# One kernel, one change: where a batch's rows are scattered to the experts' regions

## The reference, cut to what matters

```python
x = L0_attn_x                                              # (8, 1024, 256)
x = x + _layernorm(_L0_attn_ref(_layernorm(x), ...))       # linear attention per token, 16 heads of 16
x = x + _layernorm(_L0_ffn_ref(_layernorm(x), ...))        # causal attention, then a mixture of experts

# first attention, per token: q, k = elu of the projections, v
kv1 = jnp.einsum('bshe,bshd->bsed', K1, V) * SCALE         # sum over the 16 heads
w1  = jnp.einsum('bshe,bsed->bshd', Q1, kv1)               # the same for the second halves

# second part
scores = q @ k / sqrt(HD), causal mask; ctx = softmax(scores) @ v        # 16 heads, 4 key heads
h = clip(residual + ctx @ Wo); flat = rmsnorm(h)
probs = softmax(flat @ Wr); topv, topi = top_k(probs, 2)   # 2 of 8 experts for each token
moe_out = sum over the two of topv * (silu(flat @ Wg[e]) * (flat @ Wu[e])) @ Wd[e]
out = clip(h + moe_out)
```

## Time and profile before

| | us |
|---|---|
| median of 3 runs | 4165.04 (4164.26 to 4166.23) |
| the profiled execution | 4157.04 |
| its span | 4155.2 |
| PE busy | 3078.5 (74%) |
| DVE busy | 2298.0 (55%) |
| ACT busy | 1675.9 (40%) |
| POOL busy | 1106.6 (27%) |
| POOL issuing the 128 scatters of the loop | 123.7 |
| one turn of the loop (25.99 to 429.81, 429.81 to 828.58) | 403.8, 398.8 |

### The profile page before, as it was taken

How to read it: one execution, slowest core, us unless ns; L and a number is a source line. 1 busy time by engine, 2 the same in 40 slices (tenths; PEclk the granted TensorE clock), 3 DMA queues, 4 the chain that set the end, 5 groups by cost and what they waited for, 6 DMA issues and landing times. The chain is left out here.

```text
span 4155.2 us, 54042 instructions
## 1 busy us (share of the span) xinstructions
PE 3078.5 (74%) x17636; PEld 1799.8 (43%) x17637; DVE 2298.0 (55%) x4488; ACT 1675.9 (40%) x3702; POOL 1106.6 (27%) x972
## 2 busy tenths in 40 slices
PE   5588558765965696579657955885587599999991
PEld 3444434343434443443444343444343366666660
DVE  4775567466837672866386557755675122222225
ACT  2456254525542554256335624562455122222223
POOL 6310630072016202420332053106200222222222
PEclk9789789887988898889788988997789799999995
DMA  1000000000000000000000000000000533333335
GB/s 55 11 11 12 22 21 2 13 20 21 2 30 3 21 2 32 0 21 2 32 1 21 2 32 11 12 12 22 11 2 11 185 55 55 55 61 56 55 53 167
DMA packets 85960, 125.57 MB, mean 30 GB/s; under 512 B 11600, under 2 KB 70864, under 8 KB 83664
## 3 DMA queue, kind: packets, MB, share of 16 engines
q1 hardware_dynamic: 59216, 85.40, 6.5%
q0 software_dynamic: 26496, 37.01, 5.0%
HBM read 58.23 MB, written 63.36 MB: 29 GB/s over the span
## 5 line engine op out<-in xcount | busy, mean ns | idle before, releaser
L660 ACT ACTIVATE PR<-SP_ 128x512 f32<-128x512 f32 (+3 forms) x1536 | 693.8, 489 | 457.8 <-PE SP_ L1241 310.9
L925 DVE TENSOR_REDUCE NM<-MX 128x1 f32<-128x128 f32 (+7 forms) x1024 | 733.9, 752 | 231.2 <-PE MX L1210 221.0
L421 POOL DMA_INDIRECT scratch_xs<-FX,SLOT x128 | 123.7, 967 | 1467.1 <-issue 1465.5
L439 POOL TENSOR_TENSOR work<-QK,VS 128x2048 f32<-128x2048 f32 x128 | 466.6, 3670 | 136.4 <-DVE QK L774 136.2
L1238 PE MATMUL SP_<-work,KST 99*128 99x512 bf16 (+3 forms) x1536 | 469.0, 333 | 44.1 <-ACT PR L660 32.2
L1208 PE MATMUL MX<-KST,work 96*128 96x512 bf16 (+3 forms) x1536 | 442.8, 353 | 70.0 <-DVE NM L925 58.5
L1503 POOL DMA_INDIRECT scratch_h<-Y,XG x136 | 210.6, 1548 | 617.1 <-DVE Y L1566 522.9
L1544 DVE TENSOR_TENSOR AG<-UB,SL 128x512 f32<-128x512 f32 x136 | 94.0, 691 | 476.3 <-PE UB L1583 476.3
L1254 PE MATMUL OA<-PR,V 128*32 128x512 f32 (+3 forms) x3072 | 327.3, 498 | 3.3 <-ACT PR L660 3.3
L1521 ACT ACTIVATE SL<-GB 128x512 f32<-128x512 f32 x136 | 81.2, 597 | 602.3 <-PE GB L1583 602.3
L818 DVE TENSOR_REDUCE AT<-work 128x256 f32<-128x4096 f32 x64 | 282.9, 4420 | 2.2
(11 more groups left out here) (253 smaller groups left out, 5092.7 us busy)
## 6 DMA issues: line engine op xcount, KB each, us to landing
XG<-scratch_xs SPq DMA_DIRECT2D x136, 130.0 KB, 2.1
X<-in_L_attn_x SPq DMA_DIRECT2D x8, 1024.0 KB, 5.6
scratch_x<-X SPq DMA_DIRECT2D x8, 1024.0 KB, 3.9
scratch_h<-A SPq DMA_DIRECT2D x8, 1024.0 KB, 3.9
X<-scratch_x SPq DMA_DIRECT2D x16, 512.0 KB, 4.0
HH<-scratch_h SPq DMA_DIRECT2D x16, 512.0 KB, 4.5
out<-X SPq DMA_DIRECT2D x16, 512.0 KB, 3.1
wg<-in_L_ffn_Wg SPq DMA_DIRECT2D x1, 4096.0 KB, 16.7
```

What stands on the lines that cost most here:

```text
L439: sg["prod1"].by(pool.tensor_tensor(P1[t % 2][:, i * hh * D:(i + 1) * hh * D].rearrange("p (h e d) -> p h e d", h=hh, e=HD), QK[:, t % 3, ...
L660: sg["exp"].by(act.activation(PR[:, n % 8, q0:512], SP_[:, n % 2, q0:512], ACT.Exp))
L925: sg["mx"].by(dve.tensor_reduce(NM[:, qt, h:h + 1], src, AX.X, ALU.max, negate=True))
```

## The change

The loop over the 16 indirect DMAs moves, as it stands, from the head of POOL's turn to the place after the meeting at the end of phase 1. Nothing is added or removed, and the other engines' instructions are the same. Lines of the changed kernel below the old place are six lower: the products at L439 are L433 there, the scatters at L421 are L477.

```diff
             with pool.Fori(0, B) as b:
-                for t in range(NT):
-                    for j in range(2):
-                        pool.indirect_dma_start(
-                            out=dram["xs"], out_offset=bass.IndirectOffsetOnAxis(ap=SLOT[:, j, t:t + 1], axis=0),
-                            in_=FX[:, t, :], in_offset=None).then_inc(scattered, 16)
-
 
                 def gain2(u):
...
                 sg["copies"].settle(pool)
                 end_phase(pool, 1)
+
+                for t in range(NT):
+                    for j in range(2):
+                        pool.indirect_dma_start(
+                            out=dram["xs"], out_offset=bass.IndirectOffsetOnAxis(ap=SLOT[:, j, t:t + 1], axis=0),
+                            in_=FX[:, t, :], in_offset=None).then_inc(scattered, 16)
 
                 end_phase(pool, 2)
```

## The result

| comparison | before, median us | changed, median us (lowest to highest, runs) | ratio, 95% interval |
|---|---|---|---|
| the one of the record | 4166.14 (20 runs) | 4175.48 (4156.94 to 4188.63, 20) | 1.0023, 1.0012 to 1.0033 |
| again, group 3 | 4163.07 (9) | 4172.47 (4160.86 and up, 8) | 1.0020, 1.0008 to 1.0032 |
| again, group 4 | 4164.21 (12) | 4101.27 (4097.38 to 4109.83, 4) | 0.9857, 0.9841 to 0.9873 |
| again, group 5 | 4164.01 (7) | 4098.52 (4096.36 to 4100.69, 4) | 0.9839, 0.9823 to 0.9856 |

The forecast was 4102 with a range from 4094 to 4118. For the comparison on record it was wrong: 4175.48, and slower. The same kernel gave 4101.27 and 4098.52 us later, with a kernel before that takes 4163 to 4166 us everywhere.

The account below looks back on a forecast made before the run. It took the first attention to be a chain from POOL's first product, held late by the scatters; 61.6 us from that plus 1.2 from PE's clock, with 0 added in phase 2, gave 4165.04 - 62.8 = 4102, range 4094 to 4118.

Parts of the forecast that it names:

- The first product 0.08 after `QK`: Head of each turn: POOL's first product starts 0.08 after the first query-key pair ends on DVE.
- PE's wait of 11 us in all: First attention's head sum: PE's wait for POOL's product falls to some 11 us from 72.5.
- The head 62.8 shorter: Head of the turns: 61.6 us from POOL's earlier first products plus 1.2 from PE's clock, 62.8 in sum.
- the clock's 1.2: Second turn's head sum: PE's second 16 transposes run warm after a shorter wait, 1.2 us gained once.
- The casts 0.17: Phase 2: DVE's casts L931 and L935 last 0.17; a mean over 0.3 on unit 0 would indicate the lock.
- rival 1's lock: Phase 2: each of two DVE casts waits out a scatter, 15 us in all; the whole rival had chance 0.12.
- its DMA toll: Phase 2's start: unit 0's small DMAs land late, up to 21 us in all; within a rival of chance 0.12.
- rival 2: Phase 2: SP's small DMAs wait behind the scatters, 9.4 a turn lost, 12 us slower, 4177; chance 0.03.
- What is added at the new place: Phase 2's start: 20.02 us of POOL's scatters fall in idle time; cost to SP's DMAs and DVE taken as 0.
- phase 2 grows by more than 1 us: Sign for the profile after: phase 2 growing by more than 1 us would show the prediction wrong.
- so the shift goes through unchanged: First attention: the earlier first product, 61.6 us over eight turns, passes whole to the later stages.
- 0.94 for faster: Whole kernel: chance 0.94 of being faster by more than 0.2% (8.3 us) than 4165.

Follow-up runs that it names:

- group 3: Set of kernels run one after another on one chip, among them the kernel before (4163.07 us) and the changed kernel (4172.47 us).
- group 4: Later set of kernels run one after another on one chip, among them the kernel before (4164.21 us) and the changed kernel (4101.27 us).
- group 5: Last set of kernels run one after another on one chip, among them the kernel before (4164.01 us) and the changed kernel (4098.52 us).
- e13: The changed kernel again, unaltered, against the kernel before in group 4: 4101.27 us, ratio 0.9857.
- e17: The changed kernel once more, unaltered, against the kernel before in group 5: 4098.52 us, ratio 0.9839.
- e1: Kernel before with nine scatters at the turn's head, six in waits of POOL's product loop, one behind it, none in phase 2: 4108.72 us, ratio 0.9859.
- e11: Same kernel as e1, unchanged, run again in group 3: 4106.1 us.
- group 1: First set of follow-up kernels, run one after another on one chip with the kernel before (4163.9 us); the changed kernel was not run.
- e6: Kernel before with six scatters at phase 2's start and ten after the wait for the second set of SP's small DMAs: 4178.9 us.
- e10: Same kernel as e2, unchanged, run again in group 3: 4218.81 us.
- e2: Kernel before with all 16 scatters in a row later in phase 2, after the second unit's maxima are copied out: 4112.81 us, ratio 0.9864.
- e12: Kernel before with two scatters behind each of phase 2's eight sets of SP's small DMAs, run in group 3: 4123.41 us.
- e8: Kernel before, scatters kept at the turn's head, plus 16 direct whole-row transfers to an unused tensor at phase 2's start: 4172.03 us.

## Why the prediction was right at the head of the turn and wrong in its answer

**Point by point, of what was to be seen.** The first product 0.08 after `QK`: 39.08 - 38.99 = 0.09, right. PE's wait of 11 us in all: the first halves' is 8 x 1.35 = 10.8, right, but the second halves' 8 x 1.67 = 13.4 was not named; it costs nothing more, since PE is paced by POOL's halves there. The head 62.8 shorter: 141.3 - 78.5 = 62.8, right to the digit, the clock's 1.2 included, since all eight head sums take the warm 9.82. The scatters 0.96 each over 20 us: right. The casts 0.17: right. Scores 13.2 after the phase's start and no wait for `work<-MR`: 13.25, right. So rival 1's lock and its DMA toll fell, in all groups, and so did rival 2: its price (9.4 a turn) is near the loss on record, but its mechanism, SP's small DMAs behind the scatters, isn't there: `work<-MR` is waited for 2.7 us in all, as before.

**The step that failed** is the term "What is added at the new place", taken as 0. What stands there instead is that DVE and ACT wait 4 to 5 us for PE's results, and that PE's clock then stays low for longer; why PE's signals come late stays open. From the first to the second set it measured 70.7 us in the record's comparison and 68 in group 3 (229.6 - 161.8), and -1.2 in groups 4 and 5, where the 0 was right. The prediction tested two users beside the scatters, SP's transfers and DVE's port, and ended the list there. The third user is the signalling between PE and the engines that wait for it, and the row that should have been asked was not in the trace: before has scatters in a row only at the head of a turn, where POOL alone is busy for most of the time, and the ones after the loop likewise. "No row shows it" was read as 0, where by the prediction's own rule of bounds the far end was open. The test "phase 2 grows by more than 1 us" was the right one, and it hit: 8.8.

**A second step was wrong without a trace in the total**: "so the shift goes through unchanged". Of 62.8, 10 to 13 were lost before phase 2 began, in all four traces of the changed kernel. The stretch from the end of the head sum to phase 2 in the second turn, before and then e13:

```profile
460.06:630.28 170.22, 104.42 (x591) 73.81 (x589) 123.18 (x168) 73.73 (x158) 81.07 (x78) 0.84 0.04 13
```
```profile
439.37:615.41 176.04, 112.04 (x591) 80.54 (x589) 123.35 (x168) 73.84 (x158) 81.76 (x78) 0.79 0.04 13
```

The same 591 matmuls keep PE busy for 112.0 instead of 104.4 us, at a granted clock of 0.79 instead of 0.84; DVE and ACT do the same in the same time. The sixth and seventh turn lose 5 us in the same way, the third and fifth 1.5, and the first, fourth and last win 1.2 to 2.6. So PE's clock falls at other moments when the turn is shorter at its head. Why it falls at other moments was not looked into. That the forecast was still met in groups 4 and 5, to 0.7 and 3.5 us, has a second part: about 10 us gained in places that the prediction left at zero (6.8 in e13 from the eighth set on, 2.3 at the first `QK`, 1.2 between the first sets). In e13 13 us lost and 10 gained nearly cancelled, in e17 12 and 8. That was luck: the 4102 came nearer than its working had earned.

**The range and the chances.** 0.94 for faster was too sure for another reason: all cases were drawn up for one chip, with before's profile as witness for what doesn't occur. Of four comparisons of the changed kernel two came out slower by 0.2% and two faster by 1.4 to 1.6%, and nothing in before's times or profile tells which kind is being looked at.

**A version that is safe on both.** `fit` (e1, e11) leaves phase 2 alone and fills waits that POOL has in phase 1. It took 4108.72 and 4106.1 us, ratio 0.9859 and 0.986, one of them in the group in which the changed kernel took 4172.47. The changed kernel took 4101.27 and 4098.52 in groups 4 and 5, where `fit` was not run, and 66 us more than `fit` in group 3.

## What to carry to other kernels

Work that is moved into an idle engine's time has more neighbours than its data and its port: here it was the signals of an engine that shares neither. If a trace has no row with the two kinds of work side by side, the cost there is unknown and not zero, and a filling of small gaps where the two already stand together (`fit`) is worth a few microseconds of forgone gain. And before a surprising loss is explained from the kernel, run it again at another time and on a second chip: with no run of the changed kernel in group 1, the moment looked like the cause until e6 and e10.

## What the runs showed of the hardware

- The same program, beside a before that agrees to 0.1%, took 4172 or 4101 us (and e2's 4109 to 4113 or 4219), by a state of the machine that stays through a group of runs.
- In that state an engine can start on PE's result 4 to 5 us (with waits of up to 9.9 in e10) after PE's matmul has ended by the trace, while indirect scatters are issued in a row, and even with 32 bytes a row. The semaphore's rise itself is recorded late: in after 51 times, in before never. Scatters in pairs had rises up to 0.7 us late (e12). 16 direct transfers of the same rows had none (e8, one run, a row of 8.7 us).
- An indirect scatter of 128 rows takes POOL 0.96 us and starts every 1.27, a direct transfer of 128 rows 0.54.
- A wait of 4 us, 16 us into phase 2, where the clock of before and of e13 rises to full, cost about as much again (an estimate, 4.4): in the first turn of after the clock stayed at 1.2 GHz through all of the next 14 us, 8.87 of them busy.
- DVE's casts of 128 x 16 took up to 1.7 us beside POOL's memsets and 0.17 in the median beside its scatters.
